# Values kept apart from the output matrix: attention products in TensorE's two column halves, weight sums by GpSimd, output product in row halves

## The chip, the cores and the metric

The kernel runs on one core of one Trainium2 chip. TensorE multiplies into PSUM, VectorE, ScalarE and GpSimd do the work between its products, and SyncE issues the DMAs. The metric is the device time of one execution in microseconds (us); lower is better.

## The reference, cut to what matters

One gated cross-attention block and one mixture of experts, for 4 batches of 256 rows of width 128, all in float32. The part that the change touches is the attention's value path:

```
ln = layernorm(layernorm(x));  xn = layernorm(ctx) * g + b      # latents [256,128], context [256,96]
k, v = split(concat([xn @ Wkv.T, ln @ Wlkv.T]))                 # 512 keys and values, 2 heads of 64
attn = softmax(where(mask, (rms(q)*scale) @ rms(k).T, -max))    # [2 heads, 256, 512]
out  = (attn @ v).reshape(256, 128) @ Wo.T + bo
x = x + tanh(g_xattn) * out
x = x + tanh(g_ffn) * experts(layernorm(x))                     # 32 experts of 64, the best 4 by sigmoid gate
```

## The kernel before, in words

Everything fits in SBUF and each engine runs one list of stages. The orders are written out by hand in tables (`PE_ORDER`, `DVE_ORDER`, `ACT_ORDER`, `POOL_ORDER`): an entry such as `row_max 1.0` calls the function of that name with batch 1 and half 0, and every engine takes its list strictly from front to back, waiting on semaphores inside the functions. Nothing else decides the order.

For each batch b the stages are: `stats_in` and `norm_in` (both layer norms), `turn_in` (transposes), `project` (q and k), `sum_qk`, `norm_qk`, `turn_qk`, `round_qk` (normalised, transposed and rounded q and k), `row_max` (rounded scores, whose row maximum VectorE takes), `turn_max` (the maxima become rows), `weights` (transposed scores, keys on the partitions, with exp by ScalarE into `prob`; halves 0 and 1 hold two key tiles each), `attend`, `out_proj`, `stats_mid`, `norm_mid`, `turn_mid`, `select` (gates of the experts), `turn_gates`. The expert part then runs in two halves h of two batches with 16 steps c each: `up` (three rounded products), a relu and gate product by VectorE into `hid`, `split` into a rounded part (ScalarE) and a rest (VectorE), and `down` (three products that accumulate in one PSUM bank). `warm` is a product that nobody reads; 24 of them keep TensorE occupied early on.

Before the change the value weights are folded with the output matrix. `fold` forms, for each head, Wlkv_v.T @ Wo.T and Wkv_v.T @ Wo.T once. `vlat` and `vctx` multiply the normed rows by that: 256 columns for the two heads, and ScalarE copies each [128, 512] result into `vw`, in which a column of ones stands behind each head's 128 columns. `attend b.t` (t is one of two tiles of 128 queries) then makes, for each head, four accumulating products: stationary `prob` [128 keys, 128 queries], moving `vw` [128 keys, 129]. Its last column is the sum of the weights, so `out_proj` only divides and adds:

```
def attend(b, t):
    for a in range(HEADS):
        for j in range(KT):
            pe.matmul(bank_of(b, OUT + t)[:, WOA * a:WOA * a + WOA], prob[:, b % 2, a, j, P * t:P * t + P],
                      vw[:, b, j, a, :], start=(j == 0), stop=(j == KT - 1))
```

In the profile a float32 product leaves two matmul records and two weight loads; a transpose or a product of rounded operands leaves one of each. VectorE takes most stages' statistics, ScalarE empties most PSUM banks, and GpSimd (POOL) has had eight subtractions for `k_lo` and `v_lo` (`low_keys`, `low_values`), the mask and the bias.

## Time and profile before

| | us |
|---|---|
| median of 3 runs | 114.74 (113.86, 114.74, 114.76) |
| the profiled execution | 113.83 |
| its span, first to last instruction | 112.0 |
| TensorE busy | 105.6 (94%) |
| VectorE busy | 94.4 (84%) |
| ScalarE busy | 65.1 (58%) |
| GpSimd busy | 16.0 (14%) |

The profile is of one execution. What lies outside the span is 113.83 - 112.0 = 1.8 us. TensorE's busy share counts records that overlap in its pipeline, so the distance from one record's start to the next one's is what a product costs on it.

### The profile page before, as it was taken

What the parts mean: (1) busy time and instruction counts of PE and PEld (TensorE: products, weight loads), DVE (VectorE), ACT (ScalarE), POOL (GpSimd) and SP (SyncE); (2) the same over time, 40 slices, a digit from 0 to 9 for tenths busy, and PEclk for the clock granted to TensorE, in tenths of its full rate; (3) what the DMA queues carried; (4) which work ended last, traced back from release to release, by engine and by line L of the source; (5) the groups of instructions that cost most, each with busy time, mean ns of one, the idle gap of its engine ahead of it and who ended that gap; (6) DMA issues with size and microseconds to landing.
All of it is one profiled execution on the core that took longest, in us unless ns stands there. A gap on an engine that the chain in (4) does not pass through costs nothing.

```text
span 112.0 us, 2072 instructions
## 1 busy us (share of the span) xinstructions
PE 105.6 (94%) x644; PEld 85.4 (76%) x644; DVE 94.4 (84%) x307; ACT 65.1 (58%) x145; POOL 16.0 (14%) x27
## 2 busy tenths in 40 slices
PE   4999999889999999999989999999999999999990
PEld 4989889547678797768978766678888888888860
DVE  5788899779977689988596989999999799899951
ACT  4689999998989733294613502636263373644410
POOL 6000016004004666000400800000000000000000
PEclk9999999999999999999999999999999999999998
DMA  3789700000000000000003986466009985763002
GB/s 86 209 232 423 336 6 6 6 0 0 0 0 6 0 0 0 3 0 6 12 12 126 287 283 222 173 235 177 16 18 258 287 296 210 235 180 125 0 0 94
DMA packets 7111, 12.78 MB, mean 114 GB/s; under 512 B 893, under 2 KB 2557, under 8 KB 6846
## 3 DMA queue, kind: packets, MB, share of 16 engines
q1 hardware_dynamic: 7102, 12.67, 34.6%
q8 instruction: 5, 0.08, 0.3%
q14 instruction: 4, 0.03, 0.1%
HBM read 12.00 MB, written 0.66 MB: 113 GB/s over the span
## 4 chain that ended last, share of the span: by engine, by line
PE 79%; DVE 8%; ACT 7%; issue 3%; POOL 0%; DVEq 0%; POOLq 0%
PE bank L729 13%; PE bank L731 13%; PE bank L730 13%; PE bank L867 12%; PE bank L738 6%; PE bank L854 5%; PE bank L921 3%; PE bank L825 2%; DVE junk L453 2%; PE bank L852 2%; PE bank L788 2%; PE bank L813 1%; ACT cx L600 1%; PE bank L807 1%; PE bank L892 1%
## 5 line engine op out<-in xcount | busy, mean ns | idle before, releaser
L706 ACT ACTIVATE hid_hi<-keys 128x512 fp32r<-128x512 f32 x28 | 17.5, 630 | 18.5 <-DVE keys L543 15.3
L543 DVE SCALAR_TENSOR_TENSOR keys<-bank,inT 128x512 f32<-128x512 f32 x32 | 21.1, 685 | 1.3 <-issue 0.6
L560 DVE TENSOR_TENSOR hid_lo<-keys,hid_hi 128x512 fp32r<-128x512 f32 x28 | 18.7, 685 | 0.9 <-ACT hid_hi L706 0.6
L867 PE MATMUL bank<-vw,prob 128*128 128x129 f32 x128 | 15.8, 278 | 0.0
L867 PEld LDWEIGHTS bank<-vw,prob 128*128 128x128 f32 x128 | 14.8, 192 | 0.7 <-issue 0.7
L729 PE MATMUL bank<-xm_hi,k_lo 128*128 128x512 f32 x32 | 14.5, 454 | 0.0
L453 DVE CUSTOM_DVE_ANT_0 junk<-bank,mask_b 128x512 bf16<-128x512 f32 x16 | 10.4, 688 | 3.0 <-PE bank L825 3.0
L731 PE MATMUL bank<-xm_hi,k_hi 128*128 128x512 f32 x32 | 12.5, 391 | 0.0
L730 PE MATMUL bank<-xm_lo,k_hi 128*128 128x512 f32 x32 | 12.5, 390 | 0.0
L729 PE MATMUL bank<-hid_hi,v_lo 128*128 128x512 f32 x28 | 11.2, 399 | 0.0
L731 PE MATMUL bank<-hid_hi,v_hi 128*128 128x512 f32 x28 | 10.9, 391 | 0.0
L730 PE MATMUL bank<-hid_lo,v_hi 128*128 128x512 f32 x28 | 10.9, 390 | 0.0
L674 ACT ACTIVATE prob<-bank 128x512 f32<-128x512 f32 x16 | 8.6, 592 | 3.5 <-PE bank L854 3.4
L738 PE MATMUL bank<-ident 128*128 128x128 f32 x48 | 8.3, 327 | 1.5 <-POOL ident L330 1.5
L349 POOL TENSOR_TENSOR k_lo<-keys,k_hi 128x512 fp32r<-128x512 f32 x4 | 5.1, 1271 | 30.7 <-ACT k_hi L642 30.7
L738 PEld LDWEIGHTS bank<-ident 128*128 128x128 f32 x48 | 7.8, 241 | 1.7 <-POOL ident L330 1.5
L854 PE MATMUL bank<-qT,kT 64*128 64x256 f32 x64 | 9.1, 375 | 0.0
L729 PEld LDWEIGHTS bank<-xm_hi,k_lo 128*128 128x128 f32 x32 | 6.0, 188 | 2.0 <-issue 0.7
L730 PEld LDWEIGHTS bank<-xm_lo,k_hi 128*128 128x128 f32 x32 | 6.0, 189 | 1.9 <-issue 1.0
L349 POOL TENSOR_TENSOR v_lo<-values,v_hi 128x512 fp32r<-128x512 f32 x4 | 5.1, 1275 | 16.9 <-ACT v_hi L648 16.9
L731 PEld LDWEIGHTS bank<-xm_hi,k_hi 128*128 128x128 f32 x32 | 6.0, 188 | 1.3
L731 PEld LDWEIGHTS bank<-hid_hi,v_hi 128*128 128x128 f32 x28 | 5.3, 188 | 1.1
(131 smaller groups left out, 197.9 us busy)
## 6 DMA issues: line engine op xcount, KB each, us to landing
inT<-gate_rows SPq DMA_DIRECT2D x32, 256.0 KB, 4.3
keys<-keys_in SPq DMA_DIRECT2D x1, 1024.0 KB, 7.1
values<-values_in SPq DMA_DIRECT2D x1, 1024.0 KB, 9.2
out<-x_mid SPq DMA_DIRECT2D x4, 128.0 KB, 2.3
vecs_x<-x_in SPq DMA_DIRECT2D x1, 256.0 KB, 4.4
wa<-wa_in SPq DMA_DIRECT2D x1, 208.0 KB, 2.8
cx<-ctx_in SPq DMA_DIRECT2D x2, 96.0 KB, 2.7
cx<-ctx_in SPq DMA_DIRECT2D x1, 192.0 KB, 5.0
```

What stands on the lines that cost most here:

```text
L349: pool.tensor_tensor(lo[:, part], src[:, part], hi[:, part].bitcast(F32), ALU.subtract).then_inc(lo_ready, 1)
L453: dve.tensor_tensor_reduce(junk[:, n % 2, :], bank_of(b, ROW_MAX + i)[:, :], mask_b[:, b, :], 1.0, SENTINEL, ALU.add, ALU.max, mx[:, b, i ...
L543: dve.scalar_tensor_tensor(hid[:, n % 3, :], bank[H_BANK[n % len(H_BANK)]][:, :], 0.0, gated[:, n % SLOTS, :], ALU.max, ALU.mult).then_inc ...
L560: dve.tensor_tensor(hid_lo[:, m % RING, :], hid[:, n % 3, :], hid_hi[:, m % RING, :].bitcast(F32), ALU.subtract).then_inc(hid_lo_ready, 1)
L674: act.activation(prob[:, b % 2, a, 2 * i:2 * i + 2, :], head_bank(b, a)[:, :].rearrange("p (t s) -> p t s", t=2), ACT.Exp).then_inc(prob_r ...
L706: act.activation(hid_hi[:, m % RING, :], hid[:, n % 3, :], ACT.Copy).then_inc(hid_hi_ready, 1)
L729: pe.matmul(o, ll, rh, start=start, stop=False)
L730: pe.matmul(o, lh, rl, start=False, stop=False)
L731: return pe.matmul(o, lh, rh, start=False, stop=stop)
L738: pe.matmul(bank[5][:, 0:P], ident[:, :], ident[:, :], start=True, stop=True)
L854: last = pe.matmul(o[a], kT[rows[a], b, keys_t], qT[rows[a], b, :], start=False, stop=True)
L867: last = pe.matmul(bank_of(b, OUT + t)[:, WOA * a:WOA * a + WOA], prob[:, b % 2, a, j, P * t:P * t + P], vw[:, b, j, a, :], start=(j == 0) ...
```

## The change

- `fold`, `vlat` and `vctx` go. `vals b` multiplies the normed rows by the unfolded value weights (128 columns, both heads side by side): four products of 128 columns and one [128, 512] copy by ScalarE into `v`.
- `attend b` is one stage for all 256 queries. Stationary is `v` [128 keys, 64], moving is `prob` [128 keys, 256]; head 0 writes PSUM partitions 0 to 63 (the left column half of TensorE), head 1 partitions 64 to 127. The result is transposed, and ScalarE copies it into `uT` (`out_in`).
- The sums of the weights: GpSimd adds pairs of key tiles (`add_weights b.i`, two a batch, 128x512), and TensorE multiplies the pair sums with a single column of ones (`sums b`, eight products with a 128x128 stationary and one moving column). VectorE takes the reciprocals (`recips b`).
- `out b` multiplies `uT` with the scaled output matrix, head by head, each head in its row half: four products with 64 rows, 128 columns. `out_proj` is as before, but waits for it.
- GpSimd also makes the rest (`hid_lo`) for every fourth step of the expert part: 7 of the 28 `split` stages leave VectorE.
- `wb` has 128 rows of 384 columns now (65 of 704 before).
- All order tables are new. `up 0.0` now stands ahead of `attend 3`, `row_max 1.0` and `1.1` behind `weights 0.0`, and six `warm` stand ahead of `turn_in 0`, where thirteen stood.

```diff
-    warm 0, warm 1, warm 2, warm 3, warm 4, warm 5, warm 6, warm 7, warm 8, warm 9, warm 10, warm 11, warm 12,
+    warm 0, warm 1, warm 2, warm 3, warm 4, warm 5, turn_in 0, warm 6, warm 7, project 0, turn_in 1, warm 8,
...
-        vw = sb("vw", [P, B, KT, HEADS, WOA])
+        v = sb("v", [P, B, KT, HEADS * DH])
...
+        second = sb("second", [P, 2, HEADS, S])
+        first = sq[:, :, 0:KT * HEADS, :].rearrange("p b r d -> p b (r d)").rearrange("p b (a s) -> p b a s", a=HEADS)
+        uT = sq[:, :, KT * HEADS:NR, :].rearrange("p b r d -> p b (r d)")
...
+            def split(h, c):
+                n = EC * h + c
+                m = n - WHOLE
+                pool.wait_ge(hid_ready, n + 1)
+                pool.wait_ge(hid_hi_ready, m + 1)
+                if m >= RING:
+                    pool.wait_ge(down_done, n - RING + 1)
+                pool.tensor_tensor(hid_lo[:, m % RING, :], hid[:, n % 3, :], hid_hi[:, m % RING, :].bitcast(F32),
+                                   ALU.subtract).then_inc(pool_lo_ready, 1)
+
+            def add_weights(b, i):
+                pool.wait_ge(prob_ready, 2 * HEADS * b + HEADS * (i + 1))
+                pair = prob[:, b % 2, :, 2 * i:2 * i + 2, :]
+                into = first[:, b, :, :] if i == 0 else second[:, b % 2, :, :]
+                if b >= 2 and i == 1:
+                    pool.wait_ge(sums_done, b - 1)
+                pool.tensor_tensor(into, pair[:, :, 0, :], pair[:, :, 1, :], ALU.add).then_inc(pairs_ready, 1)
...
+            def recips(b):
+                dve.wait_ge(sums_done, b + 1)
+                dve.reciprocal(rsum[:, BT * b:BT * b + BT, :].rearrange("p t a -> p (t a)"), sum_bank(b)).then_inc(rsum_ready, 1)
+
             def out_proj(b):
+                dve.wait_ge(rsum_ready, b + 1)
+                dve.wait_ge(bias_ready, b // HB + 1)
+                dve.wait_ge(out_proj_done, b + 1)
...
+            def vals(b):
+                act.wait_ge(v_done, b + 1)
+                act.activation(v[:, b, :, :].rearrange("p t d -> p (t d)"), value_bank(b)[:, :], ACT.Copy).then_inc(v_ready, 1)
+
+            def out_in(b):
+                act.wait_ge(attend_done, b + 1)
+                act.activation(uT[:, b, :], att_bank(b), ACT.Copy).then_inc(u_ready, 1)
...
+            def attend(b):
+
+                pe.wait_ge(v_ready, b + 1)
                 pe.wait_ge(prob_ready, 2 * HEADS * (b + 1))
...
+                for j in range(KT):
+                    for a in range(HEADS):
+                        part = slice(DH * a, DH * a + DH)
+                        last = pe.matmul(att_bank(b)[part, :], v[:, b, j, part], prob[:, b % 2, a, j, :],
+                                         start=(j == 0), stop=(j == KT - 1))
                 last.then_inc(attend_done, 1)
+
+            def sums(b):
+                if b == 0:
+                    pe.wait_ge(ones_ready, 1)
+                pe.wait_ge(pairs_ready, 2 * b + 2)
+                pairs = (first[:, b, :, :], second[:, b % 2, :, :])
+                for t in range(BT):
+                    for a in range(HEADS):
+                        n = HEADS * t + a
+                        for i, pair in enumerate(pairs):
+                            last = pe.matmul(sum_bank(b)[:, n:n + 1], pair[:, a, P * t:P * t + P], ones[:, :],
+                                             start=(i == 0), stop=(i == 1))
+                last.then_inc(sums_done, 1)
+
+            def out(b):
+                if b == 0:
+                    pe.wait_ge(wo_ready, 1)
+                pe.wait_ge(rsum_ready, b + 1)
+                pe.wait_ge(u_ready, b + 1)
+                for t in range(BT):
+                    for a in range(HEADS):
+                        rows = slice(DH * a, DH * a + DH)
+                        last = pe.matmul(out_bank(b, a)[:, D * t:D * t + D], uT[rows, b, P * t:P * t + P], wb[rows, B_WO:B_WO + D],
+                                         start=True, stop=True)
+                last.then_inc(out_proj_done, 1)
```

TensorE's queue around the first attention product. Before, from `turn_qk 3` on (L807 and L813 are `turn_qk`, L825 `row_max`, L867 `attend`, L852 and L854 `weights`, L834 `turn_max`):

```order
L807 MATMUL bank<-ident,sq 128x128 x2
L813 MATMUL bank<-ident,sq 128x128 x4
L867 MATMUL bank<-vw,prob 128x129 x8
L825 MATMUL bank<-kT_hi,qT_hi 128x512 x2
L852 MATMUL bank<-shift_r,shift_l 128x256 x2
L854 MATMUL bank<-qT,kT 128x256 x2
L852 MATMUL bank<-shift_r,shift_l 128x256 x2
L854 MATMUL bank<-qT,kT 128x256 x2
L825 MATMUL bank<-kT_hi,qT_hi 128x512 x2
L867 MATMUL bank<-vw,prob 128x129 x8
L834 MATMUL bank<-ident_b,shift_c 97x128 x2
```

After, from the last two products of `sums 0` on (L885 is `sums`, L859 and L861 `weights`, L897 `out`, L814 and L820 `turn_qk`, L841 `turn_max`, L872 `attend`):

```order
L885 MATMUL bank<-ones,sq 128x1
L885 MATMUL bank<-ones,second 128x1
L859 MATMUL bank<-shift_r,shift_l 128x256 x2
L861 MATMUL bank<-qT,kT 128x256 x2
L859 MATMUL bank<-shift_r,shift_l 128x256 x2
L861 MATMUL bank<-qT,kT 128x256 x2
L897 MATMUL bank<-wb,sq 128x128 x4
L814 MATMUL bank<-ident,sq 128x128 x2
L820 MATMUL bank<-ident,sq 128x128 x4
L841 MATMUL bank<-ident_b,shift_c 97x128 x2
L872 MATMUL bank<-prob,v 64x256 x8
```

`turn_qk 3` stood ahead of the first `attend`; it now stands behind `attend 0`, `sums 0`, `weights 1.1` and `out 0`.

VectorE's queue at the end of the attention. Before, from `norm_mid 2` on (L496 to L501 are `norm_mid`, L487 and L490 `stats_mid`, L470 to L481 `out_proj`, L512 `turn_mid`, L543 `up`):

```order
L496 SCALAR_TENSOR_TENSOR rs_mid<-rs_mid 128x2
L497 SCALAR_TENSOR_TENSOR rs_mid<-mv_mid,rs_mid 128x2
L498 SCALAR_TENSOR_TENSOR rs_mid<-rs_mid 128x2
L501 TENSOR_SCALAR xn<-x_mid,mv_mid,rs_mid 128x128 x2
L470 RECIPROCAL rsum<-bank 128x2 x2
L476 SCALAR_TENSOR_TENSOR x_mid<-bank,rsum,x_mid 128x128 x2
L481 SCALAR_TENSOR_TENSOR x_mid<-bank,rsum,x_mid 128x128 x2
L512 TENSOR_TENSOR xm_lo<-bank,xm_hi 128x256
L487 BN_STATS bn_mid<-x_mid 128x6 x2
L490 BN_AGGR mv_mid<-bn_mid 128x2 x2
L543 SCALAR_TENSOR_TENSOR keys<-bank,inT 128x512 x3
```

After (L500 is `recips`, L520 and L523 `stats_mid`, L529 to L534 `norm_mid`, L508 and L513 `out_proj`, L545 `turn_mid`, L576 `up`):

```order
L500 RECIPROCAL rsum<-bank 128x4
L529 SCALAR_TENSOR_TENSOR rs_mid<-rs_mid 128x2
L530 SCALAR_TENSOR_TENSOR rs_mid<-mv_mid,rs_mid 128x2
L531 SCALAR_TENSOR_TENSOR rs_mid<-rs_mid 128x2
L534 TENSOR_SCALAR xn<-x_mid,mv_mid,rs_mid 128x128 x2
L508 SCALAR_TENSOR_TENSOR x_mid<-bank,rsum,x_mid 128x128 x2
L513 SCALAR_TENSOR_TENSOR x_mid<-bank,rsum,x_mid 128x128 x2
L545 TENSOR_TENSOR xm_lo<-bank,xm_hi 128x256
L520 BN_STATS bn_mid<-x_mid 128x6 x2
L523 BN_AGGR mv_mid<-bn_mid 128x2 x2
L576 SCALAR_TENSOR_TENSOR keys<-bank,inT 128x512 x3
```

`norm_mid 2` now stands behind `recips 3`, which waits for TensorE's `sums 3`.

TensorE's queue at the same place. Before, the last `attend` stages and the first experts (L892 is `turn_gates`, L867 `attend`, L875 `turn_mid`, L729 to L731 with `xm` and `k` are `up`, L729 with `sel` is `select`):

```order
L867 MATMUL bank<-vw,prob 128x129 x8
L892 MATMUL bank<-ident,gate 32x128 x2
L867 MATMUL bank<-vw,prob 128x129 x16
L875 MATMUL bank<-ident,xn 128x128 x2
L729 MATMUL bank<-xm_hi,k_lo 128x512
L730 MATMUL bank<-xm_lo,k_hi 128x512
L731 MATMUL bank<-xm_hi,k_hi 128x512
L729 MATMUL bank<-xm_hi,k_lo 128x512
L730 MATMUL bank<-xm_lo,k_hi 128x512
L731 MATMUL bank<-xm_hi,k_hi 128x512
L729 MATMUL bank<-sel_hi,xm_lo 128x32
```

After (L897 is `out`, L756 to L758 `up`, L922 `turn_gates`, L872 `attend`, L885 `sums`):

```order
L859 MATMUL bank<-shift_r,shift_l 128x256 x2
L861 MATMUL bank<-qT,kT 128x256 x2
L897 MATMUL bank<-wb,sq 128x128 x4
L756 MATMUL bank<-xm_hi,k_lo 128x512
L757 MATMUL bank<-xm_lo,k_hi 128x512
L758 MATMUL bank<-xm_hi,k_hi 128x512
L922 MATMUL bank<-ident,gate 32x128 x2
L872 MATMUL bank<-prob,v 64x256 x8
L885 MATMUL bank<-ones,sq 128x1
L885 MATMUL bank<-ones,second 128x1
```

One `up` now stands ahead of the last `attend`, and eight `sums` products and an `out` behind it.

## Rows read from the trace of the kernel before

**Rows 1.** Stretches: start:end, us, busy PE, PEld, DVE, ACT, POOL; granted clock; DMA.

```profile
16.00:24.00 8.00, 7.33 (x44) 5.53 (x42) 6.54 (x20) 7.90 (x22) 2.32 (x2) 1.00 0.02 4
...
64.00:109.00 45.00, 44.96 (x198) 35.24 (x196) 41.14 (x88) 19.57 (x35) 0.62 (x1) 1.00 0.54 172
```

**Rows 2.** TensorE in order of time: start, us, line, operands, count of records.

```profile
60.49 0.59 PE L875 MATMUL bank<-ident,xn 128*128 128x128 f32 x2
...
108.34 0.39 PE L730 MATMUL bank<-hid_lo,v_hi 128*128 128x512 f32 x1
108.57 0.39 PE L731 MATMUL bank<-hid_hi,v_hi 128*128 128x512 f32 x1
```

**Rows 3.** TensorE in order of time: `weights 0.0`, `attend 0.0`, `row_max 2.1`, `weights 1.1`.

```profile
27.59 0.28 PE L852 MATMUL bank<-shift_r,shift_l 33*128 33x256 bf16 x2
27.71 0.60 PE L854 MATMUL bank<-qT,kT 64*128 64x256 f32 x4
28.14 0.27 PE L852 MATMUL bank<-shift_r,shift_l 33*128 33x256 bf16 x2
...
35.01 1.95 PE L867 MATMUL bank<-vw,prob 128*128 128x129 f32 x16
36.89 0.50 PE L825 MATMUL bank<-kT_hi,qT_hi 64*128 64x512 f32 x2
37.23 0.28 PE L852 MATMUL bank<-shift_r,shift_l 33*128 33x256 bf16 x2
```

**Rows 4.** ScalarE in order of time, early part.

```profile
9.99 0.36 ACT L626 ACTIVATE folded<-bank 128x256 f32<-128x256 f32 x1
...
10.52 0.58 ACT L618 ACTIVATE sq<-bank 128x512 f32<-128x512 f32 x1
...
13.10 0.60 ACT L636 ACTIVATE vw<-bank 128x512 f32<-128x512 f32 x1
13.59 0.59 ACT L631 ACTIVATE vw<-bank 128x512 f32<-128x512 f32 x1
```

**Rows 5.** TensorE in order of time: `fold`, `vlat 0`, `vctx 0`.

```profile
8.31 0.39 PE L774 MATMUL bank<-wb 65*128 65x128 f32 x2
8.53 0.38 PE L775 MATMUL bank<-wb 65*96 65x128 f32 x2
...
11.17 1.03 PE L788 MATMUL bank<-folded,inT 128*128 128x256 f32 x4
12.03 1.03 PE L799 MATMUL bank<-folded,inT 96*128 96x256 f32 x4
```

**Rows 6.** TensorE in order of time: `select 0`, whose products have 32 moving columns.

```profile
49.38 0.25 PE L729 MATMUL bank<-sel_hi,xm_lo 128*128 128x32 f32 x1
49.49 0.26 PE L730 MATMUL bank<-sel_lo,xm_hi 128*128 128x32 f32 x1
```

**Rows 7.** VectorE in order of time: `select 0`'s first and last, then the attention's end.

```profile
50.41 0.22 DVE L522 TENSOR_SCALAR logit<-bank 128x64 f32<-128x64 f32 x1
...
52.35 0.22 DVE L534 SCALAR_TENSOR_TENSOR gate<-left,sig 128x64 f32<-128x64 f32 x1
...
60.61 0.23 DVE L470 RECIPROCAL rsum<-bank 128x2 f32<-128x2 f32 x2
...
63.05 1.26 DVE L543 SCALAR_TENSOR_TENSOR keys<-bank,inT 128x512 f32<-128x512 f32 x2
```

**Rows 8.** VectorE and GpSimd in order of time, at 17.6 us; GpSimd's last two.

```profile
17.65 1.02 DVE L384 SCALAR_TENSOR_TENSOR rs_in<-rs_in 128x4 f32<-128x4 f32 x1
18.71 0.16 DVE L385 TENSOR_TENSOR rs_in<-rs_in,var_in 128x4 f32<-128x4 f32 x1
...
17.62 1.04 POOL L344 TENSOR_SCALAR mask_b<-mask_u 128x1024 bf16<-128x1024 uint8 x1
...
62.10 2.52 POOL L349 TENSOR_TENSOR v_lo<-values,v_hi 128x512 fp32r<-128x512 f32 x2 [7.52 <-ACT v_hi L648]
```

**Rows 9.** TensorE in order of time: the first `warm` products.

```profile
1.50 4.88 PE L738 MATMUL bank<-ident 128*128 128x128 f32 x26 [1.50 <-POOL ident L330]
```

More of the change, by code:

```diff
@@ L33 @@
 RING = 4
+POOL_SLOT = RING - 1
 WHOLE = 4
@@ new lines @@
+    warm 0, warm 1, warm 2, warm 3, warm 4, warm 5, turn_in 0, warm 6, warm 7, project 0, turn_in 1, warm 8,
+    warm 9, vals 0, warm 10, project 1, warm 11, turn_in 2, warm 12, warm 13, turn_qk 0, warm 14, warm 15,
+    vals 1, warm 16, warm 17, warm 18, warm 19, warm 20, row_max 0.0, vals 2, warm 21, turn_in 3, warm 22,
+    warm 23, row_max 0.1, project 2, turn_qk 1, vals 3, turn_max 0, weights 0.0, row_max 1.0, turn_qk 2,
+    row_max 1.1, weights 0.1, row_max 2.0, turn_max 1, project 3, weights 1.0, row_max 2.1, attend 0, sums 0,
@@ new lines @@
+    weights 1.1, out 0, turn_qk 3, turn_max 2, attend 1, row_max 3.0, weights 2.0, sums 1, out 1, turn_mid 0,
+    weights 2.1, row_max 3.1, select 0, attend 2, sums 2, turn_max 3, turn_mid 1, weights 3.0, turn_gates 0,
+    select 1, weights 3.1, out 2, up 0.0, turn_gates 1, attend 3, sums 3, out 3, turn_mid 2, up 0.1, turn_res 0,
+    up 0.2, turn_res 1, down 0.0, select 2, up 0.3, down 0.1, turn_mid 3, up 0.4, up 0.5, down 0.2, down 0.3,
+    up 0.6, up 0.7, up 0.8, down 0.4, up 0.9, select 3, up 0.10, down 0.5, up 0.11, down 0.6, down 0.7, up 0.12,
@@ L89 @@
-    split 1.15, finish 1
+    stats_in 0, norm_in 0, stats_in 1, norm_in 1, stats_in 2, sum_qk 0, norm_in 2, norm_qk 0, stats_in 3,
+    sum_qk 1, norm_in 3, row_max 0.0, norm_qk 1, row_max 0.1, sum_qk 2, turn_max 0, scale_wo 0, norm_qk 2,
+    row_max 1.0, row_max 1.1, turn_max 1, row_max 2.0, sum_qk 3, row_max 2.1, recips 0, norm_qk 3, out_proj 0,
+    stats_mid 0, turn_max 2, norm_mid 0, recips 1, row_max 3.0, out_proj 1, turn_mid 0, stats_mid 1, row_max 3.1,
+    norm_mid 1, turn_max 3, select 0, recips 2, turn_mid 1, select 1, out_proj 2, stats_mid 2, recips 3,
@@ L90 @@
+    split 1.10, up 1.12, split 1.12, up 1.13, up 1.14, up 1.15, split 1.13, split 1.14, finish 1
 """
 ACT_ORDER = """
[L92 to L95 removed]
@@ new lines @@
+    split_values 0, sum_qk 2, round_qk 1, weights 0.0, turn_qk 2, vals 3, round_qk 2, weights 0.1, split_keys 3,
+    project 3, weights 1.0, sum_qk 3, out_in 0, split_values 1, weights 1.1, turn_qk 3, round_qk 3, stats_mid 0,
+    out_in 1, weights 2.0, turn_mid 0, weights 2.1, stats_mid 1, turn_mid 1, select 0, weights 3.0, turn_gates 0,
+    split_values 2, out_in 2, select 1, weights 3.1, turn_gates 1, split_values 3, stats_mid 2, out_in 3,
+    turn_mid 2, stats_mid 3, turn_mid 3, select 2, split 0.4, split 0.5, split 0.6, split 0.7, split 0.8,
```

229 lines of the change are left out of this document (85 added, 144 removed).

## The prediction

> **What bounds the kernel now.** I read the stretches of the span first. From 64 to 109 us TensorE is busy 44.96 of 45.00 us, VectorE 41.14 and ScalarE 19.57 [rows 1]: the expert part is TensorE's, with 0.23 us from one 512-column product to the next up to the last [rows 2]. The earlier part has two owners. From 16 to 24 us ScalarE is busy 7.90 of 8.00 us, VectorE 6.54, and TensorE 7.33 with `warm` products among its records [rows 1]: there ScalarE sets the pace. In order of time, TensorE reaches `weights 0.0` at 27.59 [rows 3]; from there to `turn_mid 2` at 60.49 [rows 2] it works nearly without a gap: adding up the distances between its records' starts leaves about 1.5 us in which it waited. So there are three questions: how much earlier does `weights 0.0` start, how much TensorE work lies behind it, and where does TensorE wait there.
>
> **An earlier start.** Ahead of `weights 0.0` ScalarE makes two `folded` copies (9.99 to 10.52, 0.53 us) and eight `vw` copies (0.49 us from start to start, 3.92 us) [rows 4]. After the change three `vals` copies stand there (1.47 us at the same 0.49) and one more `split_keys` of the same size (0.49 us). Net -0.53 - 3.92 + 1.47 + 0.49 = -2.5 us on the engine that is busy 99% of that stretch. `row_max 1.0` and `1.1` no longer come first either, on TensorE or on VectorE, so the short idle times that ScalarE had there may go too, up to 0.5 us. I take **-2.9 us** (bounds -2.0 and -3.3). TensorE's saving there, `fold` at four times 0.22 us and sixteen 256-column products at 0.43 us against sixteen 128-column ones at 0.22 us [rows 5], is 0.9 + 6.9 - 3.5 = 4.3 us, but no gain by itself: 18 of the 24 `warm` products now stand behind `turn_in 0`, eleven before, and the freed time is filled with products that nobody reads. The reshaped `wb` transfer is asked for at the same place and needed later than now: nothing.
>
> **More behind it.** `row_max 1.0` and `1.1` cost TensorE 0.34 us each [rows 3] and now lie behind `weights 0.0`: **+0.7 us**.
>
> **The attention products.** One `attend` takes 36.89 - 35.01 = 1.88 us [rows 3], eight of them 15.0 us. After, for each batch:
> - `attend`: eight products, sixteen records of 256 columns. The row-half products of `weights` have such records and take 0.43 us for four [rows 3], so they run two at a time. If column halves do the same it is 16 x 0.107 = 1.7 us, and I add 0.2 us for the first record without a partner and the change of mode: 1.9. If they don't overlap, 3.4.
> - `sums`: eight products with a 128x128 stationary and one moving column. `select` has 32 moving columns, and its records still start 0.11 us apart [rows 6], so the weight load is paid there and not the columns. A float32 product leaves two loads: 16 x 0.11 = 1.8 us, for four columns of results. Bounds 1.6 and 2.0.
> - `out`: eight loads of 128 columns and eight records of 128. One load after another it is 8 x 0.11 = 0.9 us; if the row halves also load at the same time, 0.45. The trace does not tell them apart; nearer is 0.9, since `select`'s loads are never closer than 0.11. I take 0.8.
>
> With 0.1 us between the stages that is 4.6 us a batch, 18.4 us in all: **+3.4 us** against 15.0 (bounds 4 x (1.7 + 1.6 + 0.45) - 15.0 = 0, and +4.6). What the column halves save, the sums spend: before, these were the 129th column of products that ran anyway.
>
> **Waits on TensorE behind it.** Eight products in a row became three stages that hand over to other engines twice (`out_in` by ScalarE, `recips` by VectorE). Following the new tables with the durations of the rows, TensorE arrives too early at these places:
> - `select 0` on VectorE stands behind `turn_max 3`, and that behind `sums 2` on TensorE. It takes 52.35 + 0.22 - 50.41 = 2.2 us [rows 7]; TensorE has only `turn_mid 1` (0.2 us) and `weights 3.0` (two groups of 0.55 us like that from 27.59 to 28.14 [rows 3]) ahead of `turn_gates 0`. About 0.9 us, and 0.3 us more at `select 1`.
> - At the end VectorE goes from `out_proj 3` to the first `up` in 63.05 - 60.61 = 2.4 us and needs 0.6 us for it [rows 7]. TensorE now has 3.6 us of work in that time (`turn_mid 2`, three `up` of 0.7, `select 2`, `turn_res`). After, one `up` has run ahead of `attend 3` and `select 2` comes later; some 2.1 us are left, a wait of 0.9 us at `down 0.0`. `norm_mid 2`, which ran under `attend 3.1`, stands behind `recips 3`: 0.3 us at `turn_mid 2`.
> - From `row_max 1.0` to `row_max 2.0` TensorE waits for `norm_qk 2`, VectorE's maxima and `round_qk 2` in turn: four waits of 0.3 to 0.5 us.
> - `out 1` and `out 3` wait for `recips`: 0.3 us each.
>
> They add up to some 4.5 us, 3.0 more than the 1.5 now. Such a walk puts every reply at its latest and overlooks where one wait swallows another; I take **+2.0 us** (bounds 0 and +3.5).
>
> **The expert part.** The products are the same and TensorE bounds it, so taking 7 of VectorE's 28 subtractions away buys nothing. GpSimd needs 2.52 us for two of that size [rows 8], 1.26 us each against VectorE's 0.6; what hides it is the distance from a `split` to its `down`, five or more stages in the table of TensorE. If that cover were short, each of the seven would cost up to 0.7 us. I take 0.
>
> **The sum.** -2.9 + 0.7 + 3.4 + 2.0 = +3.2 us on the profiled execution's 113.83 us (span 112.0 and 1.8 around it), 117.0 us. That execution lies 0.9 us under the median of the runs, two of which are at 114.75; I add half of it: **117.4 us**.
>
> **Rivals.**
> - *The early start wins.* Both `out` and `attend` run at their lower bounds, and the waits swallow each other: -2.9 + 0.7 + 0 + 0 = -2.2 us, 112.0 us on the same scale. Its place is the stretch from `weights 0.0` to `down 0.0`. It decides for faster when products and waits together cost less than 1.1 us, where I have 5.4. For it: row halves do run in pairs, and the orders were good for the durations before. Against: sixteen weight loads a batch for the sums, which nothing in the trace shows below 0.11 us.
> - *A draw.* The same mechanism half way, products and waits between 1.1 and 3.4 us: 113.6 to 115.9 us, middle 114.7.
> - *GpSimd holds VectorE up.* At 17.65 a VectorE instruction of 128x4 with both inputs in SBUF takes 1.02 us, where the next takes 0.16, and it ends at 18.67, as GpSimd's mask does at 18.66 [rows 8]. GpSimd now has some 15 instructions of 1.26 us in the 37 us of attention, beside six groups of such small VectorE instructions, and in the expert part its seven subtractions meet VectorE's 21: at worst 7 x 1.26 = 8.8 us on 41.1 - 4.2 = 36.9 us, more than the 45 us that TensorE takes. Price +1 to +3 us, 119.4 us. Against: GpSimd's other instructions slowed nobody down so far. The Trainium skill ("SBUF — State Buffer", Who interferes with whom) states that VectorE and GpSimd share a port pair under an exclusive lock, and that a VectorE instruction with two SBUF inputs contends with a GpSimd one that reads SBUF. By that rule this rival would be the likelier; the 1.02 us row agrees.
> - *The column halves don't overlap.* `attend` costs 3.4 us instead of 1.9; 4 x 1.5 = +6.0 us, less 1 us of waits under it: 122.4 us. Then the change doesn't do what it says. For it: the two halves need all 128 rows at once, and no product of the trace has that form. The Trainium skill ("TensorE: Matmul & The Clock Gate", Part 3) says both that weight loads overlap running products only when their rows differ, which would give this time, and that column tiles gained 2.38 times with three of them, which would give mine; no row here shows either.
> - *A slow start.* The first 26 `warm` records take 4.88 us, 0.19 us each [rows 9], where the same form takes 0.11 at 8.31 [rows 5]; with 12 records ahead of `turn_in 0` instead of 26, TensorE may stay slow longer, at about the time when ScalarE waits for it: +0.5 to +1.5 us, 118.4 us.
>
> **How the numbers follow.** Forecast 0.44, early start wins 0.11, draw 0.22, GpSimd 0.12, halves 0.06, slow start 0.05. A measurement of this kernel can tell about 1% from no change. Faster by over 1% (under 113.6): 0.11. Within 1%: 0.22. Slower: 0.67. The range from 113.5 to 120.5 us leaves out most of the first rival and the halves, under 0.2 together, and takes in the lock and most of the bounds.
>
> **What would show it.** `weights 0.0` on TensorE near 24.7 instead of 27.59. The records of `sums` 0.11 us apart, sixteen a batch; `attend` near 1.9 us a batch; `out` near 0.8. TensorE idle ahead of `turn_gates 0`, `down 0.0` and between `row_max 1.0` and `2.0`, mostly for VectorE. The distance from `down 0.0` to the last product as before, 44.4 us less `select 2`'s place. It would be wrong if the sums' records stood much closer than 0.11 us, or if the waits were as short as now.

## The result and the profile after

The changed kernel takes **124.09 us** (median of 4 executions, 123.11 to 125.66) where the one before takes 114.52 beside it: a ratio of **1.082, interval 1.077 to 1.088**. The forecast of 117.4 us had the sign and a third of the size; the range ended at 120.5. The median of the kernel before differs by up to 0.6% from chip to chip, so experiments are compared by their ratio to the kernel before, run beside each on the same chip. Three executions are left out, two of a_order (212 and 265 us) and one of the kernel before beside a_nosum (213 us): in the one of them that was profiled TensorE's 512-column products stood 0.446 us apart instead of 0.227.

The page of the changed kernel, to be held against [rows 1]: its span, the busy engines, and by fortieths of the span the busy tenths of TensorE and the clock that it was granted.

```profile
span 123.5 us, 2110 instructions
PE 113.0 (92%) x668; PEld 87.1 (71%) x668; DVE 93.7 (76%) x296; ACT 64.1 (52%) x143; POOL 35.7 (29%) x39
...
PE   5499999979998899998999899999999999999990
...
PEclk9999999999999996798559959999999999999998
```

The last line is what the prediction did not think of. The busy line is full all through, but at three places in the middle the clock is at half. The same in stretches (start:end, length, busy time of each engine, granted clock, DMA):

```profile
25.00:48.00 23.00, 20.79 (x173) 14.96 (x174) 16.91 (x55) 15.10 (x35) 12.85 (x11) 0.99 0.00 1
48.00:50.50 2.50, 2.50 (x18) 1.58 (x18) 2.27 (x9) 0.38 (x1) 0.84 (x1) 0.50 0.00 0
50.50:57.50 7.00, 6.58 (x60) 5.06 (x58) 4.58 (x20) 2.02 (x6) 1.27 (x1) 0.98 0.01 4
57.50:64.50 7.00, 6.52 (x36) 4.57 (x33) 4.09 (x21) 3.68 (x8) 1.58 (x2) 0.51 0.02 5
64.50:71.30 6.80, 6.40 (x51) 4.62 (x50) 3.61 (x17) 2.15 (x6) 2.20 (x2) 0.99 0.33 109
71.30:75.00 3.70, 3.70 (x13) 2.45 (x11) 3.56 (x13) 0.50 (x2) 0.00 (x0) 0.55 0.79 252
75.00:118.50 43.50, 43.50 (x195) 34.25 (x194) 37.03 (x75) 19.48 (x35) 10.32 (x8) 1.00 0.52 164
```

A granted clock of 0.50 is the lower of TensorE's two levels, 1.2 GHz. It is granted for some 13 us in three pieces, each of which begins within 3 us of the end of a `sums` stage (`sums 1`, `2` and `3`; none follows `sums 0`). This is the longest of the four executions; the mean clock of the others was 0.94, 0.971 and 0.966. The third piece shows why "busy" does not tell it: 3.70 of 3.70 us busy, and only 13 products in it. The kernel before shows 1.00 from 48 to 72 us.

TensorE in order of time, with the stages that answer to [rows 3] and [rows 6] (L859 and L861 `weights`, L872 `attend`, L885 `sums`, L897 `out`, L814 `turn_qk`, L951 `down 0.0`; in brackets the idle time ahead and who ended it):

```profile
25.50 0.29 PE L859 MATMUL bank<-shift_r,shift_l 33*128 33x256 bf16 x2 [0.47 <-DVE shift_r L490]
...
34.16 1.95 PE L872 MATMUL bank<-prob,v 128*64 128x256 f32 x16
36.04 0.38 PE L885 MATMUL bank<-ones,sq 128*128 128x1 f32 x2
36.28 0.36 PE L885 MATMUL bank<-ones,second 128*128 128x1 f32 x2
...
37.92 0.28 PE L859 MATMUL bank<-shift_r,shift_l 33*128 33x256 bf16 x2
...
40.64 0.44 PE L814 MATMUL bank<-ident,sq 128*128 128x128 f32 x2 [1.01 <-DVE sq L466]
...
58.82 0.61 PE L922 MATMUL bank<-ident,gate 128*32 128x128 f32 x2 [0.48 <-DVE gate L567]
...
62.79 1.06 PE L897 MATMUL bank<-wb,sq 64*128 64x128 f32 x8
63.78 0.76 PE L756 MATMUL bank<-xm_hi,k_lo 128*128 128x512 f32 x1
...
73.34 1.66 PE L951 MATMUL bank<-keys,values 128*128 128x512 f32 x2
```

`attend 0` takes 36.04 - 34.16 = 1.88 us for sixteen records of 256 columns, as forecast: the column halves run two at a time. (The Trainium skill, "TensorE: Matmul & The Clock Gate", Part 3, gives both a gain from column tiles and a rule on weight loads that would forbid it; the trace agrees with the gain.) `sums 0` takes 37.92 - 36.04 = 1.88 us, its records 0.11 us apart, as forecast. `out 2` fell in the slow clock and took 0.99 us; at full clock, in a_wide below, it is 60.23 - 59.70 = 0.53, nearer to the bound of 0.45 than to the 0.8 I took, so row halves load two at a time as well. `weights 0.0` starts at 25.50 instead of 27.59 [rows 3] (forecast 24.7), `down 0.0` at 73.34 instead of 64.45. The two rows of a_wide (`out 2` and the product behind it):

```profile
59.70 0.61 PE L898 MATMUL bank<-wb,sq 64*128 64x128 f32 x8
60.23 0.51 PE L757 MATMUL bank<-xm_hi,k_lo 128*128 128x512 f32 x1
```

### The profile page after: what moved, and what is told of

Same layout as the page of the kernel before. It is cut to its first block, busy times and chain, and to the rows that moved or that the text cites. A ratio compares the mean times of both kernels' runs of the same rounds, so it can differ in the third digit from the quotient of the medians.

```text
span 123.5 us, 2110 instructions
## 1 busy us (share of the span) xinstructions
PE 113.0 (92%) x668; PEld 87.1 (71%) x668; DVE 93.7 (76%) x296; ACT 64.1 (52%) x143; POOL 35.7 (29%) x39
## 4 chain that ended last, share of the span: by engine, by line
PE 69%; DVE 13%; ACT 9%; issue 3%; DMA 2%; POOLq 1%; DVEq 0%; ACTq 0%
PE bank L756 12%; PE bank L758 11%; PE bank L757 11%; PE bank L872 6%; PE bank L885 6%; PE bank L861 5%; PE bank L951 3%; PE bank L832 2%; DMA vecs_x<-x_in 2%; PE bank L897 2%; PE bank L786 2%; ACT hid_hi L733 2%; DVE sq L466 2%; PE bank L859 1%; DVE rs_qk L419 1%
## 5 line engine op out<-in xcount | busy, mean ns | idle before, releaser
L576 DVE SCALAR_TENSOR_TENSOR keys<-bank,inT 128x512 f32<-128x512 f32 x32 | 21.0, 683 | 3.2 <-PE bank L758 2.1
L374 POOL TENSOR_TENSOR hid_lo<-keys,hid_hi 128x512 fp32r<-128x512 f32 x7 | 9.8, 1402 | 41.5 <-ACT hid_hi L733 37.9
L593 DVE TENSOR_TENSOR hid_lo<-keys,hid_hi 128x512 fp32r<-128x512 f32 x21 | 15.2, 745 | 1.8 <-ACT hid_hi L733 1.4
L756 PE MATMUL bank<-xm_hi,k_lo 128*128 128x512 f32 x32 | 14.3, 446 | 0.0
L758 PE MATMUL bank<-xm_hi,k_hi 128*128 128x512 f32 x32 | 12.9, 403 | 0.0
L756 PE MATMUL bank<-hid_hi,v_lo 128*128 128x512 f32 x28 | 11.4, 407 | 0.2 <-POOL hid_lo L374 0.2
L861 PE MATMUL bank<-qT,kT 64*128 64x256 f32 x64 | 11.5, 441 | 0.0
L758 PE MATMUL bank<-hid_hi,v_hi 128*128 128x512 f32 x28 | 11.1, 395 | 0.0
L765 PE MATMUL bank<-ident 128*128 128x128 f32 x48 | 8.9, 327 | 1.5 <-POOL ident L347 1.5
L383 POOL TENSOR_TENSOR sq<-prob 128x512 f32<-128x512 f32 x4 | 5.1, 1266 | 14.9 <-ACT prob L701 14.9
L713 ACT ACTIVATE xm_hi<-bank 128x256 fp32r<-128x256 f32 x4 | 1.5, 384 | 14.5 <-PE bank L905 14.5
L872 PE MATMUL bank<-prob,v 128*64 128x256 f32 x64 | 7.8, 385 | 0.3 <-ACT prob L701 0.3
L756 PEld LDWEIGHTS bank<-xm_hi,k_lo 128*128 128x128 f32 x32 | 6.3, 198 | 1.8 <-DVE keys L576 0.5
L383 POOL TENSOR_TENSOR second<-prob 128x512 f32<-128x512 f32 x4 | 5.1, 1276 | 7.6 <-ACT prob L701 7.6
L758 PEld LDWEIGHTS bank<-xm_hi,k_hi 128*128 128x128 f32 x32 | 6.2, 193 | 1.5
```

The costliest lines, as they stand in the source:

```text
L374: pool.tensor_tensor(hid_lo[:, m % RING, :], hid[:, n % 3, :], hid_hi[:, m % RING, :].bitcast(F32), ALU.subtract).then_inc(pool_lo_ready, 1)
L383: pool.tensor_tensor(into, pair[:, :, 0, :], pair[:, :, 1, :], ALU.add).then_inc(pairs_ready, 1)
L576: dve.scalar_tensor_tensor(hid[:, n % 3, :], bank[H_BANK[n % len(H_BANK)]][:, :], 0.0, gated[:, n % SLOTS, :], ALU.max, ALU.mult).then_inc ...
L593: dve.tensor_tensor(hid_lo[:, m % RING, :], hid[:, n % 3, :], hid_hi[:, m % RING, :].bitcast(F32), ALU.subtract).then_inc(hid_lo_ready, 1)
L756: pe.matmul(o, ll, rh, start=start, stop=False)
L758: return pe.matmul(o, lh, rh, start=False, stop=stop)
```

## The experiments

**One column or 64 (a_wide).** What does the clock fall for, and what does it cost? (The sums' part of the bank and the input of `recips` are widened to match.)

```diff
-        ones = sb("ones", [P, 1])
+        ones = sb("ones", [P, 64])
-                            last = pe.matmul(sum_bank(b)[:, n:n + 1], pair[:, a, P * t:P * t + P], ones[:, :],
+                            last = pe.matmul(sum_bank(b)[:, 64 * n:64 * n + 64], pair[:, a, P * t:P * t + P], ones[:, :],
```

> The changed kernel with one edit: the sums multiply by 64 columns of ones instead of one (results in 256 columns of the same bank, of which every 64th is read). Sixteen weight loads a batch as before, 0.11 us each; 64 columns go under a load, so TensorE's time for the stage stays 1.8 us. Theory 1 (the granted clock falls to its lower level because one-column products leave the array unused): the clock stays at 1.0 from 47 to 75 us, the span falls by 4 to 6 us, time near 119 us. Theory 2 (the clock falls because TensorE waits for VectorE and ScalarE there): waits and clock stay as they are, time within 1 us of the changed kernel's 124.1 us.

Measured: 121.18 us, four executions within 0.12 us, ratio 1.060 (1.056 to 1.064). As many instructions, at the same distance (pairs of records at 52.79, 53.06 and 53.29 us), each with 64 times the columns:

```profile
span 119.0 us, 2110 instructions
...
PEclk9999999999999999999999999999999999999999
```

Theory 1 was right on the clock and in the span of the profiled executions (4.5 us less); the time stayed 2 us above its 119, because the profiled execution of the changed kernel was the longest of its four. So the low clock is worth 2.3% of 114.5, **2.6 us** between the medians and 4.5 us between the two profiled executions, and products that load 128 columns of weights to use them on one column bring it about here. (The Trainium skill, same page, "HAM oscillation", ties the fall to gaps in which TensorE is idle. Between 41.7 us and the first fall it was held up once, for 0.28 us ahead of `out 1`, so the rows of this fall disagree, and a_wide has the same gap, 0.27 us, at the same place and keeps its clock. Gaps do it as well, see a_order2.)

a_wide is the changed kernel without the low clock, and its stretches can be set against those of the kernel before: first a_wide from `weights 0.0` to `down 0.0` and from there to the end,

```profile
25.50:69.43 43.93, 39.77 (x329) 28.50 (x330) 31.91 (x123) 23.39 (x57) 18.71 (x15) 1.00 0.09 31
69.43:119.00 49.57, 46.21 (x201) 35.57 (x201) 39.46 (x82) 19.47 (x35) 11.06 (x8) 1.00 0.52 157
```

then the kernel before, the same two.

```profile
27.59:64.45 36.86, 35.99 (x301) 29.25 (x300) 29.88 (x124) 21.26 (x52) 10.48 (x9) 1.00 0.11 35
64.45:112.00 47.55, 44.51 (x196) 34.87 (x194) 41.58 (x88) 19.57 (x35) 0.17 (x1) 0.99 0.52 165
```

The first stretch grew by 7.07 us: 3.78 more busy, and 4.16 us idle against 0.87, 3.29 more. The second grew by 2.02 us.

**The sums left out (a_nosum).** The attention output is then not divided by its sums; all waits for GpSimd's additions stay.

```diff
-                dve.wait_ge(sums_done, b + 1)
-                dve.reciprocal(rsum[:, BT * b:BT * b + BT, :].rearrange("p t a -> p (t a)"), sum_bank(b))
+                dve.wait_ge(pairs_ready, 2 * b + 2)
+                dve.reciprocal(rsum[:, BT * b:BT * b + BT, :].rearrange("p t a -> p (t a)"), ones[:, :])
```

with `sums 0` to `sums 3` taken out of TensorE's order.

> The changed kernel with the sums of the weights left out: TensorE's one-column products are gone, and VectorE takes its reciprocals of a constant one, once GpSimd's pair sums are there (the attention output is so not divided by its sums). Everything else stands, GpSimd's additions and the waits for them too. Theory A, the sums are work on the path: 4 batches of 1.88 us, 7.5 us, and the 2.9 us that the low clock cost (a_wide) go from the ratio 1.0824, so 0.99 of the kernel before (113.7 where that takes 114.6). Theory B, the sums hid ScalarE's copy of the attention output and GpSimd's additions: TensorE now waits at the output products of each batch (0.5 us for the copy, more where GpSimd is late), 0.5 to 1.5 us a batch, and its clock may fall there: 1.01 to 1.04. Each tells how much of the loss against the kernel before the sums carry: there the sums came with the value products, as their 129th column.

Measured: 114.28 us, ratio **0.997 (0.993 to 1.001)**. The first stretch:

```profile
26.18:63.75 37.57, 32.39 (x265) 21.34 (x266) 31.39 (x122) 23.30 (x57) 18.69 (x15) 1.00 0.08 23
```

Busy time falls by 7.38 us against a_wide and the idle time grows by only 1.0 (5.18 against 4.16), with the clock at its upper level in this stretch. Theory A holds, with 0.997 for its 0.99; theory B's waits were nearly all there already. Of the 8.5% between the changed kernel and this one, 6.3 are the sums' own time and 2.3 the clock that they cost: everything else in the change comes to nought. The earlier start and the cheaper attention product pay for the waits and the rest.

**Warm-up products (a_warm, a_both, b_start).** a_warm puts seven of the `warm` products back ahead of `turn_in 0`, a_both does so in a_wide, b_start takes them away from there in the kernel before (lines of its table, cut short):

```diff
-    warm 5, warm 6, warm 7, warm 8, warm 9, warm 10, warm 11, warm 12,
-    turn_in 0, warm 13, warm 14,
+    warm 5, turn_in 0, warm 6,
+    warm 7, warm 8, warm 9, warm 10, warm 11, warm 12, warm 13, warm 14,
```

> The changed kernel with thirteen warm products ahead of turn_in 0 again (seven moved forward, 24 in all as before). Theory 1 for the start (with six, TensorE stands idle from 4.4 to 6.4 us and its clock rises at 9.8 us instead of 5.1): project 0 takes 0.9 instead of 1.7 us, weights 0.0 starts near 24.7 instead of 25.5, time 0.5 to 1 us lower, the low stretches at 47 to 75 us stay in size but may move. Theory 2 (the start is hidden by ScalarE's queue): no change at weights 0.0, time within 0.5 us.

> Both edits: 64 columns of ones, thirteen warm products at the start. If the clock is the whole surprise, what is left over the kernel before is the recorded sum without it: 117 to 118 us, +2.5 to +3.5 us over the kernel before. If something else was missed (contention on VectorE, the pace of 512-column products, 0.231 instead of 0.227 us), it stays above 119 us.

> The kernel before with only six warm-up products ahead of turn_in 0 in place of thirteen (the seven others behind it), as the changed kernel has it. Theory A: the start up to weights 0.0 is bound by VectorE's and ScalarE's chain, so TensorE's slower start (turn_in 0 took 1.16 us in the changed kernel, 0.75 in the one before) costs 0.4 us at most: 114.6 to 115.0. Theory B: TensorE bounds its start in the kernel before (the chain of waits runs over it from 1.5 to 13.1 us), so the later rise of its clock costs 1 us or more: 115.6 or above. Its profile also tells whether the 512-column products of the expert part stand 0.227 us apart (a property of the kernel before) or 0.231 as in every run of the changed kernel (a property of this chip).

Measured: a_warm 1.082 (1.076 to 1.088) and a_both 1.060 (1.054 to 1.065), each where it was without the move, and a_both above the 119 us that its expectation set as the sign of something else missed; `weights 0.0` starts at 25.23 and 26.00 against 25.50 without it. The slow start costs the changed kernel nothing that can be measured, and that rival falls. The profiled execution of a_both also shows that 64 columns do not rule a fall out: just behind the wait of 0.81 us at `turn_gates 0` the clock was at half for 3.4 us, where a_wide with the same wait kept it.

```profile
58.90:62.30 3.40, 3.40 (x23) 2.61 (x22) 2.00 (x11) 1.65 (x5) 0.62 (x1) 0.50 0.04 10
```

b_start: 117.61 us, 1.031 (1.027 to 1.035), theory B (115.6 or above). TensorE in b_start:

```profile
6.38 0.69 PE L746 MATMUL bank<-ident,xn 128*128 128x128 f32 x2 [1.95 <-DVE xn L423]
...
7.29 4.84 PE L738 MATMUL bank<-ident 128*128 128x128 f32 x26
11.96 0.39 PE L774 MATMUL bank<-wb 65*128 65x128 f32 x2
...
31.23 0.28 PE L852 MATMUL bank<-shift_r,shift_l 33*128 33x256 bf16 x2
```

`fold 0` starts at 11.96 instead of 8.31 [rows 5], and `weights 0.0` 3.64 us later than at 27.59: the whole of it comes through. As many records stand ahead of `fold` as before, but TensorE now waits 1.95 us for `turn_in 0` with 12 of them done, and of the 26 behind it 17 stand 0.21 us apart, the rest 0.11; in the kernel before 12 stand there, 0.11 us apart. It shows that TensorE bounds the start of the kernel before, where `fold` stands ahead of `project 0`, and, with a_warm, that it does not bound the start of the changed one.

**All splits on VectorE (a_dvesplit).** GpSimd's seven subtractions go back to VectorE, as in the kernel before (one stretch of VectorE's table).

```diff
-    split 0.8, select 3, split 0.9, up 0.11, up 0.12, split 0.10, up 0.13, up 0.14, split 0.12, up 0.15,
+    split 0.7, up 0.10, split 0.8, select 3, split 0.9, up 0.11, up 0.12, split 0.10, up 0.13, split 0.11, up 0.14, split 0.12, up 0.15,
```

> The changed kernel with all 28 split stages on VectorE again, each put back behind its predecessor. Theory 1 (the expert part is TensorE's, GpSimd's part hidden): expert part from down 0.0 on within 0.5 us, except the 0.6 us that the last down waits for GpSimd. Theory 2 (GpSimd and VectorE hold each other up on two-input subtractions, and that slows the expert part): 1 to 3 us faster. The 512-column products' distance of 0.231 us returns to 0.227 only if GpSimd's traffic causes it.

Measured: 123.39 us, 1.077 (1.071 to 1.083); the interval overlaps that of the changed kernel, so the time alone settles nothing. The profile does: `down 0.0` to the end is 123.6 - 74.48 = 49.1 us where the changed kernel has 123.5 - 73.34 = 50.2 and a_wide, without the low clock at its beginning, 49.6. Half a microsecond, theory 1; the 512-column products kept their distance of 0.231 us. VectorE's splits in the changed kernel, then GpSimd's (min, median, max in ns; first and last start in us), and VectorE's in a_dvesplit:

```profile
L593 DVE TENSOR_TENSOR hid_lo<-keys,hid_hi x21: 674/683/1194, 80.8 to 117.2; 128x512 fp32r<-128x512 f32 x21
...
L374 POOL TENSOR_TENSOR hid_lo<-keys,hid_hi x7: 1291/1294/1557, 83.5 to 117.9; 128x512 fp32r<-128x512 f32 x7
```

```profile
L592 DVE TENSOR_TENSOR hid_lo<-keys,hid_hi x28: 681/684/693, 81.3 to 118.6; 128x512 fp32r<-128x512 f32 x28
```

With GpSimd beside it VectorE's median is unchanged, and a few instructions are held, one to 1.19 us. In the expert part the rival of GpSimd holding VectorE up is worth 0.5 us at most. No run takes GpSimd's additions out of the attention, and there the rows show more. In a_wide, TensorE's longest wait (0.96 us, `turn_qk 3`), and ahead of it VectorE's `norm_qk 3` and GpSimd's `add_weights 1.0`:

```profile
40.63 0.44 PE L815 MATMUL bank<-ident,sq 128*128 128x128 f32 x2 [0.96 <-DVE sq L466]
```

```profile
38.45 1.19 DVE L419 TENSOR_TENSOR rs_qk<-rs_qk,ms 128x12 f32<-128x12 f32 x1
```

```profile
38.35 1.26 POOL L383 TENSOR_TENSOR sq<-prob 128x512 f32<-128x512 f32 x1
```

VectorE's instruction takes 0.17 us in the other batches; here it ends at 39.64, with GpSimd's at 39.61. It stands on the chain of waits that leads to the end of the kernel. Without its 1.02 us too much the wait would be gone (an estimate). The profiles of the changed kernel, a_warm, a_dvesplit and a_pad have it at the same place.

**The places of the buffers (a_pad).** In the expert part, where no product changed, the 512-column products stood 0.231 us apart on average instead of 0.227, in a_dvesplit too. a_pad is a_wide with two unused buffers:

```diff
+        sb("pad0", [P, 768])
         bo = sb("bo", [P, D])
...
+        sb("pad1", [P, 1056])
         x_mid0 = sb("x_mid0", [P, NT, D])
```

> a_wide (the changed kernel with sums over 64 columns of ones) with two unused buffers among its declarations, so that every buffer of the expert part has the place in SBUF that it has in the kernel before. No instruction differs from a_wide. In every run of the changed kernel the 512-column products of the expert part stand 0.230 to 0.232 us apart, in both runs of the kernel before 0.226 to 0.227. Theory A, the places of the buffers cause it: the distance returns to 0.227 and the time falls by 180 products of 0.0045 us, 0.8 us, below a_wide (1.0597 of the kernel before), to about 1.053. Theory B, it is something else (the 64-row products ahead of it, GpSimd's splits): the distance stays at 0.231 and the ratio at 1.060.

Measured: 120.74 us, 1.061 (1.053 to 1.070); two executions at 120.3, two at 121.1 and 122.1, so the time can't tell. The trace can. The stretch from `down 0.0` on and the durations of the third product of each `up`, in a_pad:

```profile
69.23:118.10 48.87, 45.60 (x201) 35.36 (x201) 39.44 (x82) 19.48 (x35) 11.06 (x8) 0.99 0.51 162
```

```profile
L761 PE MATMUL bank<-xm_hi,k_hi x32: 388/389/402, 60.6 to 109.4; 128*128 128x512 f32 x32
```

and in a_wide:

```profile
L759 PE MATMUL bank<-xm_hi,k_hi x32: 389/393/404, 60.8 to 110.1; 128*128 128x512 f32 x32
```

The distance is back at 0.227, theory A. It is not the chip: a_order2 ran on a_pad's chip without the padding and has 0.231. 48.87 instead of 49.57 us: 0.7 us of the change's cost comes from where in SBUF the expert part's buffers happened to move when `folded` and `vw` went. Which distance between addresses matters isn't shown.

**VectorE's order (a_order, a_order2).** The longest waits of a_wide were 0.96 us at `turn_qk 3` and 0.81 at `turn_gates 0`, both for VectorE. Three swaps in its order (parts of the lines of its table):

```diff
-recips 0, norm_qk 3, out_proj 0
+norm_qk 3, recips 0, out_proj 0
-turn_max 3, select 0, recips 2
+select 0, turn_max 3, recips 2
-recips 3, norm_mid 2, out_proj 3
+norm_mid 2, recips 3, out_proj 3
```

> The changed kernel with sums over 64 columns of ones (as in a_wide) and three swaps in VectorE's order: norm_qk 3 ahead of recips 0, select 0 ahead of turn_max 3, norm_mid 2 ahead of recips 3. Nothing else differs from a_wide (121.2 us). Theory A, the waits that VectorE's order adds are real time: in a_wide TensorE waited 0.96 us at turn_qk 3, 0.81 at turn_gates 0 and 0.33 at select 0, so at best 2.1 us go; what is late next gives part of it back, so 119.5 to 120.3. Theory B, the waits only move: norm_qk 3 and select 0 hold up what they are put ahead of (row_max, out_proj 0, weights 3.0), and the time stays within 0.4 us of 121.2.

> The same kernel as a_order, since its profiled execution had TensorE at half speed throughout and tells nothing of the waits. Its two other executions took 122.9 and 123.0 us at a mean clock of 0.98, 2 us above what a_wide's ratio gives on that chip (120.7). Theory A: VectorE's swaps shorten the waits at turn_qk 3 and turn_gates 0 but a stretch of low clock (2 per cent of 120 us at half speed, 1.2 us lost) takes it back. Theory B: the waits only moved, to row_max 3.0, out 0 and out 3, by more than they were shortened. The profile tells: 4.2 us of idle TensorE between weights 0.0 and down 0.0 in a_wide; A has 2.5 or less there, B 4 or more.

Measured: a_order 1.078 (1.073 to 1.083), a_order2, the same kernel again, 1.077 (1.072 to 1.082), 1.7% above a_wide, which neither of a_order's theories had. TensorE in a_order2, around the second swap:

```profile
55.01 0.39 PE L906 MATMUL bank<-ident,xn 128*128 128x128 f32 x2
57.30 0.39 PE L860 MATMUL bank<-shift_r,shift_l 33*128 33x256 bf16 x2 [1.90 <-DVE shift_r L490]
57.48 1.06 PE L862 MATMUL bank<-qT,kT 64*128 64x256 f32 x4
```

and two stretches of the same kernel, from `weights 0.0` to `down 0.0` and the ten microseconds behind that wait:

```profile
26.20:74.78 48.58, 43.97 (x330) 31.37 (x330) 32.20 (x123) 23.17 (x57) 18.71 (x15) 0.89 0.08 29
```

```profile
57.30:67.30 10.00, 10.00 (x51) 6.86 (x53) 4.37 (x21) 4.35 (x11) 3.77 (x3) 0.50 0.01 3
```

By a_order2's own measure, 4 us idle or more, theory B, with the low clock of theory A beside it. The waits at `turn_qk 3` and `turn_gates 0` are gone, but `weights 3.0` now waits 1.90 us for `turn_max 3`, and TensorE's idle time is 48.58 - 43.97 = 4.6 us where a_wide has 4.2. On top of it the clock is at its lower level for ten microseconds behind the wait; in the kernel's other executions, with a mean clock of 0.98, for some four (0.017 x 120.8 / 0.5), which is worth the 2 us that a_order2 lies above a_wide (an estimate from the mean clock).

**The sums the other way round (e_statr, e_stato, e_ln).** If the price is weight loads used on one column, let the ones be the weights and the pair sums move.

```diff
-                            last = pe.matmul(sum_bank(b)[:, n:n + 1], pair[:, a, P * t:P * t + P], ones[:, :],
+                        last = pe.matmul(sum_bank(b)[DH * a:DH * a + DH, :], ones[:, :], pair[:, a, :],
...
-                act.activation(uT[:, b, :], att_bank(b), ACT.Copy).then_inc(u_ready, 1)
+                then(dve.reciprocal(rs_u[:, b % 2, :], sum_bank(b)))
+                dve.tensor_tensor(uT[:, b, :], att_bank(b), rs_u[:, b % 2, :], ALU.mult).then_inc(u_ready, 1)
```

> The changed kernel with the sums made the other way round: 64 columns of ones are the weights and the pair sums move (four products of 256 columns for a batch, in the two column halves), so the sums come out in the layout of the attention output; VectorE takes the reciprocal of 256 columns and multiplies the attention output by it (in place of ScalarE's copy), the output product contracts over all 128 rows (two products of 128 columns, no halves), and VectorE adds its result to the residual in one instruction. Theory A, the price is TensorE's work: sums 0.94 us for a batch (half of the 1.88 of attend 0, which has twice the products) in place of 1.88, output product 0.44 in place of 0.55, so 4.2 us less than a_wide (121.2) for four batches: 117.0, and the clock stays at its upper level. Theory B, the output product now stands behind a longer chain on VectorE (reciprocal and product, some 0.4 us each for 256 columns, where a reciprocal of 4 columns stood), so up to 0.8 us for a batch come back as waits: 117 to 120. If the clock falls nevertheless, 2 to 3 us more.

> e_statr with the three swaps of a_order in VectorE's order. If VectorE's order is what TensorE waits for, 1 to 2 us below e_statr; if the waits only move, within 0.4 us of it. Below 114.6 would beat the kernel before.

> e_statr with the reciprocal of the sums made by ScalarE (logarithm, then the exponential of its negative) in place of VectorE's reciprocal, which took 1.75 us for 256 columns; VectorE multiplies the attention output by it. out 1 stands behind weights 2.1 and out 3 behind up 0.1, and VectorE's steps for them one or two places later, so that the longer chain lies beside other work. Theory A, products of few instructions pay once the chain is covered: sums 0.94 us and output product 0.44 for a batch, 1.0 less than in a_wide, so 4 us below a_wide: a ratio of 1.02 to 1.03. Theory B, ScalarE's and VectorE's chain (0.4 + 0.4 + 0.4 us behind the sums of each batch) is waited for and the clock falls in those waits: 1.05 or more.

Measured: e_statr 1.155 (1.148 to 1.162), e_stato 1.164 (1.156 to 1.173), e_ln 1.062 (1.057 to 1.067). TensorE's part came out as reckoned, 38.02 - 37.05 = 0.97 us a batch:

```profile
37.05 0.60 PE L872 MATMUL bank<-sq,ones 128*64 128x256 f32 x4
37.48 0.60 PE L872 MATMUL bank<-second,ones 128*64 128x256 f32 x4
38.02 0.28 PE L848 MATMUL bank<-shift_r,shift_l 33*128 33x256 bf16 x2
```

VectorE's did not: 256 columns of reciprocal take four times what their product takes. In e_statr,

```profile
L501 DVE RECIPROCAL rs_u<-bank x4: 1745/1754/1758, 38.9 to 72.8; 128x256 f32<-128x256 f32 x4
L502 DVE TENSOR_TENSOR sq<-bank,rs_u x4: 424/424/426, 40.7 to 74.6; 128x256 f32<-128x256 f32 x4
```

and TensorE waited 6.8 us for it in three places, with the mean clock at 0.93. The three swaps on top (e_stato) did not help, the two intervals overlap; TensorE's waits at the same places were 9.3 us. With ScalarE's logarithm and exponential instead, and `out 1` and `out 3` some places later (e_ln), e_statr's loss is gone and nothing is won over a_wide: one wait of 2.74 us stands where `turn_mid 1` is queued on VectorE behind the multiplication of batch 2, and the clock falls for 6.8 us behind it:

```profile
56.70 0.36 PE L750 MATMUL bank<-sel_hi,xm_lo 128*128 128x32 f32 x1 [2.74 <-DVE xm_lo L537]
```

None of the versions beats the kernel before.

## Why the prediction was wrong

The sign was right, and for the forecast's reason, the sums as work of their own (a_nosum); the size was not. Term by term, from the stretches of a_wide, the low clock apart (`select 2`, 0.67 us, moved from the first stretch to the second, is put back):

| term | forecast | measured |
|---|---|---|
| start of `weights 0.0` | -2.9 | -2.1 |
| `row_max 1.x` and attention products | +4.1 | 3.78 + 0.67 = +4.4 |
| waits of TensorE behind `weights 0.0` | +2.0 | 4.16 - 0.87 = +3.3 |
| expert part | 0 | 2.02 - 0.67 = +1.4 |
| sum, clock at its upper level | +3.2 | +7.0 (119.0 against 112.0) |
| low clock | not in it | +2.6 between the ratios, +4.5 in the profiled execution |

**The step that failed** is one that is not there: every product was priced at its distance in a trace whose clock never fell, and no rival asked whether sixteen weight loads for a single column would keep TensorE at its upper level. They did not; that is shown by a_wide. It is 2.6 of the 6.7 us missing, the largest of the errors but not enough alone: the start gives 0.8, the products 0.3, the waits 1.3, the expert part 1.4, and the last 0.3 is that the runs beside the result had a lower median than the one the forecast started from. Without the low clock the time would be 121.4 us (1.060 of 114.52), above the range as well.

**The waits** were mis-sized by a place that the walk had left out. The walk through the tables gave 3.0 us, and I cut it to 2.0 on the general ground that such a walk overstates. For its own places that was right: `turn_gates 0` 0.81 (forecast 0.9), `down 0.0` 0.68 (0.9), `out 1` and `out 3` 0.54 together (0.6), 0.33 for `select`, at `select 0` instead of 1 (0.3), nothing that the profile marks as a wait at `turn_mid 2` (0.3), and of the four waits between `row_max 1.0` and `2.0` one of 0.26. Together 2.6 us where the walk had some 4.5; less the 0.7 us of marked waits in the kernel before that is 1.9, close to the 2.0. What broke the sum is 0.96 us at `turn_qk 3`, which was not in the walk; the rest is short idle times of no named cause. Two things meet there. `norm_qk 3` stands on VectorE behind `recips 0`, which waits for `sums 0`: the same mechanism as at `select 0`, which I had seen. And GpSimd's addition holds it up by 1.02 us (a_dvesplit above): the rival that the sum had at nothing. Either alone may be harmless: with `norm_qk 3` put first (a_order2) it is held as long and TensorE doesn't wait there. That VectorE's order can't simply be turned round is a_order2's lesson, `turn_max 3` being late next.

**The start** was worth 2.1 instead of 2.9. ScalarE had less to do there as reckoned, but the chain of waits of the changed kernel between 5 and 17 us goes mostly through VectorE (`xn`, the statistics, `sq`), then mostly over TensorE, and only from 23 us on through ScalarE. One of VectorE's pieces, at 16.6 us, took 0.68 us beside GpSimd's mask, where the kernel before has 0.17. The bound of 2.0 held; the value taken assumed that the engine that was the slowest stays the only one.

**The expert part** was not free. 0.7 us is the places of the buffers (a_pad); 0.5 us is GpSimd's splits (a_dvesplit; one wait of 0.2 us on `hid_lo` stands in the trace, the rest is spread); 0.2 us I can't place. The prediction named GpSimd's cover as the condition and took it as given. Where the buffers lie it did not consider.

**The products** were right: `attend` 1.88 (1.9), `sums` 1.88 (1.8), `out` 0.53 (0.8, with 0.45 as a bound). The rivals: the column halves do overlap; GpSimd's hold on VectorE is real, 0.5 us at most in the expert part and by the rows up to 1 us at `turn_qk 3` and 0.5 in the start, together within the 1 to 3 us it was given, of which only the first was put to a test; the slow start is there (`turn_in 0` 1.16 us instead of 0.75) and hidden. The range failed because its rivals were taken one at a time, where clock, waits and expert part all went the same way.

What carries the loss is the sentence "what the column halves save, the sums spend": without the sums the kernel stands at 0.997.
